# A fused Mamba block and fp8 linear layer on one core: one group of states is multiplied by C on GpSimd, in the layout of the scan

## The reference

```
x = x + LN(block(LN(x)))                 # LN: layernorm without weights
x = x + LN(fp8(LN(x)) @ fp8(W_ffn).T + b)

block(r):
  xz = r @ W_in + b_in;  x_in, z = halves of xz             # 256 inner features each
  xc = silu(causal depthwise conv over 4 taps of x_in)
  B, C = halves of xc @ W_xp + b_xp                         # 16 states each
  delta = softplus(xc @ W_dt + b_dt);  A = -exp(A_log)
  h[t] = exp(delta[t] * A) * h[t-1] + delta[t] * xc[t] * B[t]     # per feature and state
  y[t] = sum over the 16 states of h[t] * C[t]
  y = (y + D_skip * xc) * silu(z)
  out = y @ W_out + b_out;  return weighted LN(r + out)
```

## Time and profile before

| what | value |
|---|---|
| median of 3 runs | 593.94 us (593.66 to 595.33) |
| the profiled execution | 596.42 us, of which the trace spans 594.7 us |
| mean granted TensorE clock | 0.918 of full |
| one slot in the middle, start to start | 64.2 us |
| busy in the span | PE 512.0, DVE 502.9, ACT 433.9, POOL 351.0 us |

### The profile page before, as it was taken

The page is one execution under the profiler, slowest core; times in us unless marked ns, Lnnn a source line. Parts: engine busy times, 40 slices in busy tenths (PEclk is TensorE's granted clock), DMA queues, the critical chain, the costliest instruction groups (busy, mean ns, idle before and its releaser), DMA issues.

```text
span 594.7 us, 9011 instructions
## 1 busy us (share of the span) xinstructions
PE 512.0 (86%) x2875; PEld 397.1 (67%) x2875; DVE 502.9 (85%) x1013; ACT 433.9 (73%) x870; POOL 351.0 (59%) x327
## 2 busy tenths in 40 slices
PE   6989899998899989997999889988999879765292
PEld 4557686877687767876687758676877668655030
DVE  5167699988998998889898899898789999987786
ACT  2558994999579965999399949995699958730264
POOL 3054364948577674948394858676585759530154
PEclk8989999999899889998899999998999899878555
DMA  7201633053505360434304350535042514460018
GB/s 185 63 1 23 121 69 74 11 98 72 106 2 107 62 115 2 76 62 85 64 15 94 72 107 1 106 73 107 0 89 54 107 35 81 78 127 0 1 35 196
DMA packets 19918, 41.21 MB, mean 69 GB/s; under 512 B 3744, under 2 KB 10016, under 8 KB 19872
## 3 DMA queue, kind: packets, MB, share of 16 engines
q0 software_dynamic: 9936, 34.87, 31.1%
q1 hardware_dynamic: 9936, 5.78, 3.7%
HBM read 3.68 MB, written 2.10 MB: 10 GB/s over the span
## 4 chain that ended last, share of the span: by engine, by line
PE 52%; DVE 20%; ACT 12%; POOL 8%; issue 5%; DMA 0%; DVEq 0%; POOLq 0%; ACTq 0%
PE drive L1078 16%; PE hT L1095 11%; PE fbank L1021 8%; DVE state L1301 8%; PE fbank L1036 4%; PE drive L1075 3%; DVE acc_d L1324 3%; ACT term L828 3%; POOL u L538 3%; PE fbank L1113 2%; ACT nrm L718 2%; PE drive L1021 2%; ACT L771 2%; POOL state L687 1%; PE fbank L1105 1%
## 5 line engine op out<-in xcount | busy, mean ns | idle before, releaser
L1301 DVE TENSOR_TENSOR_SCAN state<-decay,drive 128x512 f32<-128x512 f32 x256 | 297.5, 1203 | 28.2 <-ACT decay L807 12.2
L807 ACT ACTIVATE decay<-delta,a_neg 128x510 f32<-128x510 f32 x256 | 171.3, 729 | 23.8 <-DVE state L1301 22.0
L1095 PE MATMUL hT<-ident,state 128*128 128x128 f32 x1024 | 148.8, 282 | 22.2 <-DVE acc_d L1324 13.8
L1078 PE MATMUL drive<-diag,uT 128*128 128x256 f32 x640 | 165.0, 405 | 0.8 <-DVE uT L1503 0.8
L1095 PEld LDWEIGHTS hT<-ident,state 128*128 128x128 f32 x1024 | 122.9, 146 | 49.5 <-ACT term L828 16.0
L1078 PEld LDWEIGHTS drive<-diag,uT 128*128 128x128 f32 x640 | 125.5, 206 | 20.2 <-issue 3.4
L828 ACT ACTIVATE term<-hT,Ct 128x256 f32<-128x256 f32 x256 | 102.5, 483 | 4.9 <-PE hT L1095 4.9
L550 POOL TENSOR_TENSOR scaled<-uT,Bt 128x1024 f32<-128x1024 f32 x48 | 95.8, 1996 | 5.9 <-DVE uT L1503 4.2
L565 POOL TENSOR_SCALAR_AFFINE_SELECT diag<-Bt 128x512 f32<-128x512 f32 x80 | 59.1, 793 | 35.4 <-PE drive L1078 17.6
L581 POOL DMA_DIRECT2D acc<-term x64 | 61.6, 967 | 18.5 <-issue 9.5
L1324 DVE SCALAR_TENSOR_TENSOR acc_d<-hT,Ct,acc_d 128x256 f32<-128x256 f32 x160 | 66.6, 471 | 5.3 <-PE hT L1095 5.3
(11 more groups left out here) (190 smaller groups left out, 661.6 us busy)
## 6 DMA issues: line engine op xcount, KB each, us to landing
acc<-term POOLq DMA_DIRECT2D x64, 512.0 KB, 4.8
out_dram<-x_all SPq DMA_DIRECT2D x7, 256.0 KB, 3.0
x_all<-term POOLq DMA_DIRECT2D x5, 256.0 KB, 3.9
x_all<-in_L_attn_x_dram SPq DMA_DIRECT2D x2, 256.0 KB, 4.0
state<-in_L_attn_conv_w_dram SPq DMA_DIRECT2D x1, 512.0 KB, 5.9
w_in<-in_L_attn_W_in_dram SPq DMA_DIRECT2D x1, 256.0 KB, 4.7
w_dt<-in_L_attn_W_dt_dram SPq DMA_DIRECT2D x1, 256.0 KB, 4.5
out_dram<-x_all SPq DMA_DIRECT2D x2, 128.0 KB, 2.7
```

The source lines that it names most:

```text
L807: last = nc.scalar.activation(decay[:, g % DECAYS, h, :, s, 1:], delta[:, par, h, :, 1:], ACT.Exp, scale=a_neg[:, h, SG * g + s:SG * g + s ...
L1078: last = nc.tensor.matmul(dst[:, :, P * c:P * c + P], uT[:, par, TC * b + c, P * h:P * h + P], diag[:, n % DIAGS, c, :, :], start=True, st ...
L1095: last = nc.tensor.transpose(hT[:, ring(n, c), DI * s + P * h:DI * s + P * h + P], state[:, n % STATES, h, s, P * c:P * c + P], ident[:, :])
L1301: nc.vector.tensor_tensor_scan(state[:, n % STATES, h, :, :].rearrange("p s t -> p (s t)"), decay[:, g % DECAYS, h, b, :, :].rearrange("p ...
```

## The change

Group 6 (units 12 and 13) leaves DIRECT and becomes PLACED. Its states are not turned and VectorE does not multiply them. Instead SyncE stores C of that group to a small table in HBM (`c_rows`), as 4-byte elements, and loads it back to every partition (`c_all`, 128 x 1024 elements, 512 KB). GpSimd multiplies the states of a unit by it (`product`, 128x1024) and adds the two states (`acc_p`, 128x512). In `back_y` VectorE adds `acc_p` to each half of y, and only then is the half marked ready. To make room in SBUF several buffers are shared or held once (`acc_d`, `h2`, `xq` and others). GpSimd now prepares B two units ahead in place of three, unit 14 in place of 15 is prepared by `scale_u`, and many steps stand at other places.

```diff
-LEAD = 3
+LEAD = 2
-DIRECT = (3, 6, 7)
+PLACED = (6,)
+DIRECT = (3, 7)
+LAG_P = 3
-MUL_U = (2, 6, 8, 10, 12, 15)
+MUL_U = (2, 6, 8, 10, 12, 14)
-POOL_STEPS = dict(front_root=(2,), front_residual=(31,), front_u=(25,), back_gate=(9,), back_affine=(18,),
-                  back_sum=(25,), sum_states=(5,), back_root=(15, 22, 25))
+POOL_STEPS = dict(front_root=(3,), front_residual=(25,), front_u=(25,), back_gate=(10,), back_affine=(20,),
+                  back_sum=(25,), sum_states=(5,), back_root=(17, 24, 28))
...
+            def spread_c(pr, par):
...
+                    sp.dma_start(c_rows[k].rearrange("r p -> p r"),
+                                 Ct[:, par, SG * g:SG * g + SG, :].rearrange("p s j -> p (s j)"), **slow)\
+                        .then_inc(c_stored[k], 16)
...
+                    sp.dma_start(c_all[:, :, :, :].rearrange("p s b t -> p (s b t)"),
+                                 c_rows[k].rearrange("(o r) p -> o (r p)", o=1).to_broadcast([P, SG * TOK]))\
+                        .then_inc(c_spread[k], 16)
...
+            def place_c(pr, par, n):
...
+                pool.wait_ge(c_spread[k], nth(pr, 16, 16))
+                pool.wait_ge(scan_done, nth(pr, 2 * UNITS, 2 * n + 2))
...
+                nc.gpsimd.tensor_tensor(product[:, :, :, :], state[:, n % STATES, :, :, :],
+                                        c_all[:, :, b, :].unsqueeze(1).to_broadcast([P, HALVES, SG, L]), ALU.mult)\
+                    .then_inc(product_ready, 1)
...
+                nc.gpsimd.tensor_tensor(total, product[:, :, 0, :], product[:, :, 1, :], ALU.add).then_inc(placed_done, 1)
...
             def transpose_states(pr, par, n, c):
+                if n // PAIR in PLACED:
+                    return
...
             def back_y(pr, par, h):
...
-                                               in1=back_bank(pr, h), op0=ALU.mult, op1=ALU.add).then_inc(y_ready, 1)
+                                               in1=back_bank(pr, h), op0=ALU.mult, op1=ALU.add).then_inc(y_part, 1)
+                dve.wait_ge(placed_done, nth(pr, PLACES, PLACES))
+                dve.wait_ge(y_part, nth(pr, 2, h + 1))
+                nc.vector.tensor_tensor(yv[:, h, :], yv[:, h, :], acc_p[:, h, :, :].rearrange("p b t -> p (b t)"), ALU.add)\
+                    .then_inc(y_ready, 1)
```

More of the change, by code:

```diff
@@ L60 @@
 LAG_T, LAG_C, LAG_A = 2, 3, 4
-LEAD = 3
+LEAD = 2
 DECAY_LEAD = 1
 DECAYS, DIAGS, STATES, TERMS = 2, 4, 4, 4
-DIRECT = (3, 6, 7)
-SCALED_G = tuple(g for g in range(DS // SG) if g not in DIRECT)
+PLACED = (6,)
+DIRECT = (3, 7)
+SCALED_G = tuple(g for g in range(DS // SG) if g not in DIRECT + PLACED)
+TURNED_G = tuple(g for g in range(DS // SG) if g not in PLACED)
+TURNED = PAIR * len(TURNED_G)
+PLACES = PAIR * len(PLACED)
+LAG_P = 3
 SCALED_N = PAIR * len(SCALED_G)
@@ L125, in ring_before @@
         return 0, (q - RING) // TC, (q - RING) % TC
-    q = max(k for k in range(TC * UNITS) if k % RING == q)
+    q = max(k for k in range(TC * units) if k % RING == q)
     return -1, q // TC, q % TC
@@ L245, in build_sandwich @@
         acc = sb("acc", [P, 2, PAIR, TC, SG, DI])
-        acc_d = sb("acc_d", [P, 2, PAIR, TC, DI])
+        acc_d = sb("acc_d", [P, PAIR, TC, DI])
+        acc_p = sb("acc_p", [P, HALVES, PAIR, L])
+        product = sb("product", [P, HALVES, SG, L])
+        c_rows = nc.dram_tensor("c_rows", [len(PLACED), PAIR * SG * TC, P], F32, kind="Internal").ap()
+        c_all = sb("c_all", [P, SG, PAIR, L])
         yv = sb("yv", [P, HALVES, TOK])
@@ L346, in build_sandwich @@
         drive_ready = sem("drive_ready")
+        sp_waited = sem("sp_waited")
+        c_stored = [sem("c_stored_%d" % k) for k in range(len(PLACED))]
+        c_spread = [sem("c_spread_%d" % k) for k in range(len(PLACED))]
+        product_ready = sem("product_ready")
+        placed_step = sem("placed_step")
+        placed_done = sem("placed_done")
+        y_part = sem("y_part")
         scan_done = sem("scan_done")
@@ L1082, in transpose_states @@
             def transpose_states(pr, par, n, c):
+                if n // PAIR in PLACED:
+                    return
                 if c == 0:
                     pe.wait_ge(scan_done, nth(pr, 2 * UNITS, 2 * n + 2))
-                back, old_n, old_c = ring_before(n, c)
+                t = turn(TURNED_G, n)
+                back, old_t, old_c = ring_before(t, c, TURNED)
+                old_n = unit(TURNED_G, old_t)
                 if not back or pr.after(1):
```

103 lines of the change are left out of this document (71 added, 32 removed).

## The result

The changed kernel takes **619.38 us** (median of 4, 619.07 to 620.86) against 593.80 us before (592.89 to 595.33): ratio 1.043, 95% interval 1.041 to 1.046. The forecast was 599.1 us with a range of 585 to 603. The sign was right, the size was not, and the time lies outside the range.

The account below looks back on a forecast made before the run. No engine alone bounds the kernel; the chain changes engine. Terms sum to +1.1 us per pair, +6.6 over six steps, -1.8 first slot, -1.0 last, +1.45 epilogue: +5.2, 599.1 us from the median, range 585 to 603.

Parts of the forecast that it names:

- y, on the chain: In back_y, two serial VectorE adds of acc_p, 0.74 us each, delay POOL's gate: +1.45 us per pair.
- y against POOL: The first add of y waits for POOL's scaled and ends late: +0.75 us per pair, bounds 0 and 1.4.
- End of the slot: Without transposes and acc_d of units 12 and 13, bshift to drive takes 2.65 us, not 4.55: -1.9 per pair.
- The norm: The norm stands earlier on ACT, so DVE's wait goes: -0.4 us; bvar no longer meets a diag: -0.45.
- front_low: VectorE's dt_e ends late behind POOL's SBUF reads: +0.6 us per pair, bounds 0 and 1.3; sign: dt_e above 1.2 us.
- Hidden work: POOL's two products (2.37 us each) and sums, less xnb, 5.8 us, fit in 7.2 us idle at the seam.
- front_delta: VectorE's delta waits while POOL runs xnb, moved there: +1.05 us per pair, bounds 0 and 1.3.
- First slot: The first slot has no back and loses 16 transposes: -1.8 us.
- Last slot: The last slot has no front: +2.2 us for y, -3.2 for acc_d, together -1.0.
- Zero, and so for the two units' lead: Preparing B two units ahead instead of three was priced at zero.
- Store and load have most of a slot. Zero: C's store (upper bound 21 us) and load have nearly 60 us of a slot, so cost zero.
- POOL is the limit at the seam: Rival: product and sum take 5 us a unit, making sum_states and PE 1.3 us late six times, 607 us; 8%.

Follow-up runs that it names:

- e6: Changed kernel with GpSimd's product and its sum cut to 4 of 256 time steps, transfers, waits and order kept: 611.14 us (1.031).
- e7: Changed kernel with GpSimd's preparation of unit 12 moved directly behind unit 11's, ahead of the add that waits for ScalarE: 605.89 us (1.019).
- e9: Changed kernel with the 4-byte store of C held back until both products of the pair before are made: 613.12 us (1.032).
- e13: Changed kernel with unit 11 multiplied on GpSimd (scaled) and unit 12 spread (diag), instead of the other way round: 605.84 us (1.018).
- e8: Kernel before with LEAD 2 and unit 14 instead of LEAD 3 and unit 15, its own tables of steps kept: 611.17 us (1.027).
- e12: Kernel before with LEAD 2 and unit 14, and unit 12 prepared right behind unit 11, ahead of the norm and the add: 589.12 us (0.992).
- e3: Changed kernel with LEAD 3 and unit 15 in place of LEAD 2 and unit 14, new tables kept: 626.12 us (1.050).
- e10: Changed kernel with y's SBUF-only part (xc times D plus acc_p) done ahead of VectorE's wait for TensorE's bank: 606.83 us (1.021).
- e14: Changed kernel with unit 12 prepared ahead of the add, C's store held back, D's part of y early, and the old tables of steps: 597.05 us (1.005).

## Why the prediction was wrong, by its own steps

**Right.** *y, on the chain* and *y against POOL*: +1.45 and +0.75 were forecast, the way to the gate grew by 2.29, the first add takes 1.40 us behind `scaled`, and TensorE's output projection starts 7.03 us after the first read (387.56) instead of 4.77. *End of the slot*: 2.65 us from `bshift` to the drive forecast, 2.76 in the trace (358.45 to 361.21). *The norm* and `bvar` behind it: no wait, 0.17 us. *`front_low`*: 1.22 us, "above 1.2". *Hidden work*: product and sum are hidden in the steady slots (e6), though the product took 2.67 us and not 2.37. *`front_delta`*: 2.25 us in three of six slots, and in all six with the row mended (e7). *First slot* -1.8: with the store out of the way (e9) the first y comes 1.9 us earlier than before (whose profiled execution was 2.6 us over its median). *Last slot* -1.0: -0.8.

**Wrong, the step "Zero, and so for the two units' lead".** This is the step that failed most. The forecast put a shorter lead at nothing without listing what the moved rows come to stand behind. The lead is also a place in a queue: with 2 for 3, `scaled` of unit 12 moves behind the add of unit 5's terms, which waits 3.52 us for ScalarE's term. With the tables of the kernel before it moves behind the norm, which waits 8.58 us for ScalarE. Mending it brings 13.5 us here (e7, and e13 by another way), of which 2.7 lie at the first seam, and 22 us in the kernel before (e8 to e12). The prediction had the rule in hand, an instruction of VectorE that waits for GpSimd's, and applied it to `dt_e`, `delta`, `bvar` and the add of y. It left out the first `bshift`, with its two SBUF inputs the most exposed of all, where GpSimd idled 7.95 us before. The lead and the new tables together filled that gap: with the lead alone (e8) GpSimd still idles 8.58 us there, with the new tables and a lead of 3 (e3) only a short diag stands behind the add, and in both `bshift` takes its 0.16 us.

**Wrong, the step "Store and load have most of a slot. Zero".** True of their own time. What was not asked is whom the store meets: it runs beside accumulating transfers, whose wait stands on GpSimd's queue ahead of the product. It costs 6.3 us in the changed kernel (e9, by medians), nearly all at the first seam; where the transfers were slowed less (e7, e10), less is left to gain. In a later slot the store is issued at 352.68 and the next of these transfers at 355.15, 2.5 us later and not 1.3, and the wait of the add at the seam is 1.75 us (365.39) and holds no scan. In the next slot the add waits 1.32 us (431.33) and a scan behind the product 1.25 (436.49); e9 has neither.

**Half wrong, `front_delta`, +1.05.** In two of six slots `delta` takes 1.20 us and in one 1.51: in the slot shown the scans ahead of it wait 1.11 us for a late drive, and `xnb` is through. Where the row is mended the meeting is there in all six. The mechanism was right and its premise, that all else stays on time, held in half of the slots.

**Sizes.** The part behind the last y: +1.45 forecast, +2.4 in the table; from the last read to the end of both halves' gate pass 4.45 us in place of 2.86, so the adds are 1.6 of it, and the other 0.8 is not traced. The slot's first `bvar`, which the forecast left as it was, took 0.90 us in place of 0.18; and in the first slot `dt_e` and `delta` took 2.27 and 2.40 us in place of 1.00 and 1.19. Put together: 599.1 forecast, plus 13.5 for the row and 6.3 for the store, makes 618.9 against 619.4 measured. That this comes out so close is luck. The two gains overlap by 2.7 us at the first seam, `delta` was forecast some 3 us too dear (three of six slots), and the sixth slot some 3 us too cheap.

**The rivals.** "POOL is the limit at the seam" gave 607 and is not what happened: e6 leaves the steady slots as they are. Of the things named as proof against the forecast one came true, that a scan waits for a product. The long wait, 5.08 us, is behind a slow transfer, not for want of GpSimd's time; two more, of 1.3 us each, come at later seams, and the last of them has no waiting add ahead of it.

**Open.** The stretch from the 6th to the 7th y varies from 59.7 to 66.8 us over these kernels, without following any one edit. In e14, with all three mended, it is 65.0, of which one wait for a product is 3.7. How much of the row's 13.5 us is the blocked `bshift` itself, how much the lower clock behind it and how much the first seam wasn't separated either; nor was the blocked `bvar` of e8 from TensorE's wait.

## What to carry to other kernels

A number that says how far ahead work is prepared is also a place in an in-order queue. Before it is priced at nothing, list what stands directly ahead of the moved row and what *that* waits for, and which short instruction of VectorE will run beside it; the queue's idle time before says nothing on either. Price a small transfer by its neighbours: ask who runs on the same DMA engines in its few us, and what is queued behind their completion. An operation that needs only SBUF, on a chain that waits for a PSUM bank, belongs ahead of the wait. And mend the order before judging a change of the work: here one row cost about half of what the change lost.
